# The gated layer of a four-layer transformer kernel: the logistic function in one ScalarE operation

## What is computed

```python
x1 = x + attn_out
h2 = _rms_norm(x1, ln2_w)
mlp = jax.nn.silu(h2 @ w_gate) * (h2 @ w_up) @ w_down
processed = x1 + mlp
gate = jax.nn.sigmoid(sel_scores).reshape(S, 1)
gated = gate * processed + (1.0 - gate) * x
output = hidden_states.at[b, idx].set(gated.reshape(B, k, D))
```

## Time and profile before

| | us |
|---|---|
| median of 3 runs | 1667.61 |
| the runs | 1668.44, 1667.61, 1667.5 |
| the profiled execution, its own time | 1672.15 |
| span of the profiled execution | 1670.3 |
| stage around the change, in that span | about 791 to 822 |

### The profile page before, as it was taken

How to read it: one execution, slowest core, us unless ns; L and a number is a source line. 1 busy time by engine, 2 the same in 40 slices (tenths; PEclk the granted TensorE clock), 3 DMA queues, 4 the chain that set the end, 5 groups by cost and what they waited for, 6 DMA issues and landing times. The chain is left out here.

```text
span 1670.3 us, 26603 instructions
## 1 busy us (share of the span) xinstructions
PE 1495.2 (90%) x8478; PEld 1012.7 (61%) x8540; DVE 1264.9 (76%) x3430; ACT 1108.1 (66%) x2384; POOL 1087.1 (65%) x1281
## 2 busy tenths in 40 slices
PE   7899999999999767987748999999999999987998
PEld 4334434434434236756646888878888888776675
DVE  5688788888888239642659999999999999873433
ACT  2146666666766737122238999999999999994332
POOL 6205566566565572131448999999999999963353
PEclk9779999999999979999979999999999999999999
DMA  5301001001000033821000000000000100000000
GB/s 202 114 21 39 21 21 39 21 21 40 21 22 20 2 129 109 318 101 51 0 1 1 1 1 1 1 1 1 1 1 1 51 1 1 1 1 1 1 26 26
DMA packets 39812, 59.84 MB, mean 36 GB/s; under 512 B 9132, under 2 KB 33592, under 8 KB 38776
## 3 DMA queue, kind: packets, MB, share of 16 engines
q1 hardware_dynamic: 39528, 56.03, 10.0%
q10 hardware_dynamic: 144, 2.10, 0.3%
HBM read 40.93 MB, written 16.78 MB: 35 GB/s over the span
## 5 line engine op out<-in xcount | busy, mean ns | idle before, releaser
L610 ACT ACTIVATE a_PT<-a_sc 128x512 f32<-128x512 f32 x576 | 317.7, 600 | 187.7 <-PE a_sc L678 128.4
L515 DVE TENSOR_REDUCE a_mpart<-a_nat 128x1 f32<-128x512 f32 (+3 forms) x640 | 364.3, 628 | 78.1 <-PE a_nat L645 41.0
L2057 DVE BATCH_NORM_STATS2 c_stat<-c_R 128x6 f32<-128x512 f32 x576 | 381.3, 680 | 2.0 <-ACT c_R L1976 2.0
L2021 POOL TENSOR_SCALAR c_R<-big,c_negtau 128x256 f32<-128x256 f32 x264 | 300.7, 1164 | 32.1 <-DVE c_negtau L2090 27.1
L2021 POOL TENSOR_SCALAR c_R<-c_Z,c_negtau 128x256 f32<-128x256 f32 x255 | 290.5, 1165 | 19.7 <-DVE c_negtau L2123 18.7
L642 PE MATMUL a_nat<-mem 96*128 96x512 bf16 (+3 forms) x768 | 243.6, 345 | 21.1 <-DVE a_mpart L515 10.9
L1893 PE MATMUL c_z<-mem,c_R 128*128 128x256 f32 x1024 | 231.9, 380 | 0.0
L482 POOL TENSOR_SCALAR_AFFINE_SELECT a_PT<-a_PT 128x512 f32<-128x512 f32 x128 | 79.0, 636 | 221.6 <-ACT a_PT L610 221.6
L1976 ACT ACTIVATE c_R<-c_Z,c_negtau 128x256 f32<-128x256 f32 x513 | 215.6, 513 | 0.4 <-DVE c_negtau L2123 0.4
L1976 ACT ACTIVATE c_R<-big,c_negtau 128x256 f32<-128x256 f32 x504 | 212.5, 514 | 3.1 <-DVE c_negtau L2090 1.7
L1893 PEld LDWEIGHTS c_z<-mem,c_R 128*128 128x128 f32 x1024 | 193.4, 190 | 25.6
(11 more groups left out here) (316 smaller groups left out, 2470.5 us busy)
## 6 DMA issues: line engine op xcount, KB each, us to landing
mem<-qk_parts SPq DMA_DIRECT2D x360, 32.0 KB
qk_parts<-a_parts SPq DMA_DIRECT2D x16, 384.0 KB, 2.6
made<-f_made SPq DMA_DIRECT2D x24, 256.0 KB, 2.8
mem<-made SPq DMA_DIRECT2D x3, 2048.0 KB, 7.8
X<-in_L_attn_x_dram SPq DMA_DIRECT2D x4, 512.0 KB, 6.9
mem<-in_L_ffn_wq_dram SPq DMA_DIRECT2D x1, 2048.0 KB, 14.9
ternary<-f_W_T ACTq DMA_DIRECT2D x1, 2048.0 KB, 8.3
mem<-in_L_ffn_wo_dram SPq DMA_DIRECT2D x1, 2048.0 KB, 14.1
```

The source lines that it names most:

```text
L515: dve.tensor_reduce(mpart[:, b, j:j + cnt, i, k0 // 512], src, AX.X, ALU.max).then_inc(s_max, 1)
L610: act.activation(PT[:, n % 3, c, :], sc[:, u % 2, :], ACT.Exp, scale=SCALE0).then_inc(s_exp, 1)
L2021: pool.tensor_scalar(split(i, h) if r < NR else whole(i, h), scores_of(i)[:, h, :], threshold(i, r, h), 0.0, ALU.add, ALU.max).then_inc(s_ ...
L2057: dve.bn_stats(stat[:, r, b, :], R[:, slot(i), b, :]).then_inc(s_stat, 1)
```

## The change

Unit by unit, ScalarE copies the up half first and then computes sigmoid(gate) into e1. GpSimd's addition and VectorE's reciprocal are gone, with the semaphore `s_one`. VectorE multiplies e1 by the gate into e2, and waits for product u-2 before it writes e2 again. GpSimd only makes the product with sq. The token gate gg is one Sigmoid of the router's scores; gs and its two VectorE operations are gone. The order on TensorE is the same.

```diff
@@ gpsimd
-            def one_more(u):
-                pool.wait_ge(s_eg, u + 1)
-                pool.tensor_scalar(e2[:, u % 2, :], e1[:, u % 2, :], 1.0, None, ALU.add).then_inc(s_one, 1)
-
-            one_more(0)
-            one_more(1)
             for u in range(FF1 // P):
                 pool.wait_ge(s_gate, u + 1)
                 pool.wait_ge(s_up, u + 1)
                 pool.tensor_tensor(mT[:, u, :], e2[:, u % 2, :], sq[:, u % 2, :], ALU.mult).then_inc(s_m, 1)
-                if u + 2 < FF1 // P:
-                    pool.wait_ge(s_m, u + 1)
-                    one_more(u + 2)
@@ vector
                 gate = big[:, u % 4, 0:S]
-                dve.wait_ge(s_one, u + 1)
-                c.link(dve.reciprocal(e2[:, u % 2, :], e2[:, u % 2, :]))
-                dve.wait_ge(s_up, u + 1)
-                dve.tensor_tensor(e2[:, u % 2, :], e2[:, u % 2, :], gate, ALU.mult).then_inc(s_gate, 1)
+                dve.wait_ge(s_eg, u + 1)
+                if u >= 2:
+                    dve.wait_ge(s_m, u - 1)
+                dve.tensor_tensor(e2[:, u % 2, :], e1[:, u % 2, :], gate, ALU.mult).then_inc(s_gate, 1)
 
             dve.wait_ge(s_eg, FF1 // P + 1)
-            c.link(dve.tensor_scalar(gs1[:], gs[:], 1.0, None, ALU.add))
-            c.link(dve.reciprocal(gg[:], gs1[:]))
             c.link(dve.tensor_scalar(gs1[:], gg[:], -1.0, 1.0, ALU.mult, ALU.add))
@@ scalar
-                act.activation(e1[:, u % 2, :], big[:, u % 4, 0:S], ACT.Exp, scale=-1.0).then_inc(s_eg, 1)
                 act.activation(sq[:, u % 2, :], big[:, u % 4, S:2 * S], ACT.Copy).then_inc(s_up, 1)
+                act.activation(e1[:, u % 2, :], big[:, u % 4, 0:S], ACT.Sigmoid).then_inc(s_eg, 1)
...
-            act.activation(gs[:], XS[:, :, D], ACT.Exp, scale=-1.0).then_inc(s_eg, 1)
+            act.activation(gg[:], XS[:, :, D], ACT.Sigmoid).then_inc(s_eg, 1)
```

More of the change, by code:

```diff
@@ L1324, in routed_ffn @@
         turned = mT[:].rearrange("p (e k) s -> p e k s", e=2)
-        gs, gs1, gg = sb("b1_gs", [P, B]), sb("b1_gs1", [P, B]), sb("b1_gg", [P, B])
+        gs1, gg = sb("b1_gs1", [P, B]), sb("b1_gg", [P, B])
         go = sb("b1_go", [P, B, D])
@@ L1331, in routed_ffn @@
         (s_sq, s_rs, s_h, s_tr, s_hT, s_qk, s_t, s_rope, s_v, s_vc, s_s, s_mx, s_nb, s_ex, s_rd, s_pn, s_pt, s_ptc, s_o, s_oc,
-         s_y, s_x1, s_gu, s_eg, s_dv, s_m, s_pool, s_out, s_tab, s_rot, s_et, s_etc, s_up, s_one, s_gate) = (
-            sem("b1_" + n) for n in ("sq rs h tr hT qk t rope v vc s mx nb ex rd pn pt ptc o oc y x1 gu eg dv m pool out tab rot et etc up one gate").split())
+         s_y, s_x1, s_gu, s_eg, s_dv, s_m, s_pool, s_out, s_tab, s_rot, s_et, s_etc, s_up, s_gate) = (
+            sem("b1_" + n) for n in ("sq rs h tr hT qk t rope v vc s mx nb ex rd pn pt ptc o oc y x1 gu eg dv m pool out tab rot et etc up gate").split())
         block = ctx.enter_context(nc.Block())
```

## The result

| | kernel before | changed kernel |
|---|---|---|
| median, lowest to highest (22 runs each) | 1669.44 us, 1667.40 to 1673.64 | 1666.43 us, 1665.31 to 1669.30 |
| span of the profiled execution | 1670.3 us | 1664.0 us |

The ratio of changed to before is 0.9982, 95% interval 0.9976 to 0.9988: 3.0 us less, 2.0 to 4.0. It is faster beyond the interval, but less than the 0.2% that the prediction took as its bound, so by that bound it is "same". The time of 1666.43 us lies 0.13 us above the range. Note the first column: the three runs shown ahead of the prediction had a median of 1667.61 us, the 22 runs have 1669.44.

A forecast was written before the change was run, and what follows sets the result against it. TensorE stalls behind the slower elementwise chain bounded the gated part; 1.37 + 0.14 + 0.12 + 1.95 = 3.58 us would go, leaving TensorE the bound. Off the 1667.61 us median this gave 1664.0 us, range 1662.0 to 1666.3.

The forecast's parts named there:

- the 0.2% that the prediction took as its bound: Whole kernel: a measurement can tell about 0.2%, 3.3 us, from no change; the forecast gain lay only just beyond it.
- The sum in the stage: Gated part and down product: TensorE stalls of 1.37, 0.14, 0.12 and 1.95 us all go, 3.58 us together.
- one load of 1.28 us between Copy and Sigmoid: ScalarE, first unit of the gated loop: a second function table is loaded, bounds 0 and 1.28 us, 1.28 taken.
- hidden up to 2.9 us: Before unit 4 on TensorE: a table load of up to 2.9 us is covered by TensorE's own work.
- the forecast 815.80: After the down product: VectorE's tail starts at 815.80 us instead of 819.38, earlier by 3.58.
- the same 3.58 us off the median gives 1664.0 us: Whole kernel: the stall sum of 3.58 us taken from the median of 1667.61 us gives the forecast time.
- The low stretches move with the work: TensorE's clock, as at the scatter product: assumed that low-clock stretches shift along with the work.
- a round of 4.1 us over two buffers: Gated loop: exponential, addition, reciprocal and two products form a round over two buffers, about 2.25 us a unit.
- a load back: Rival, after the gated part: the old table is reloaded on the path, at most 1.28 us, 1665.3 us; chance 0.08.
- tables to and fro: Rival, ScalarE in the gated loop: two loads in every unit, 2.57 us, giving 1674.6 us; chance 0.04.
- an elementwise chain that is hidden anyway: Rival, gated part: the change does nothing because that chain is already covered, 1667.6 us; chance 0.01.
- The clock rival: Rival, scatter product or similar pauses: clock gives or takes 1.7 us, 1662.3 or 1665.7 us; chance 0.10 for both ends.

The follow-up runs named there:

- e4: Changed kernel with the logistic function made by Tanh of half the gate, 1 added in VectorE's multiply; median 1667.40 us, ratio 0.9974 to the kernel before.
- e6: Changed kernel with a two-column Sigmoid and Exp before the first Sigmoid, so three table loads there; ratio 0.9974 to the kernel before.
- e2: Changed kernel with VectorE's reciprocal kept and only GpSimd's addition gone; ratio 0.9994 to the kernel before, stretch 22.74 us.
- e10: Kernel before (Exp, addition and reciprocal) with four buffers for e1, e2 and sq; ratio 0.9998 to the kernel before, stretch 23.69 us.
- e3: Changed kernel with an addition (of zero) kept on GpSimd and only the reciprocal gone; ratio 0.9998 to the kernel before, stretch 22.21 us.
- e9: Changed kernel with GpSimd's addition kept and four buffers for e1, e2 and sq; ratio 0.9974 to the kernel before, stretch 19.29 us.
- e5: Changed kernel with a two-column Exp after each unit's Sigmoid, 16 table loads in the gated part; ratio 1.0049 to the kernel before, stretch 31.86 us.
- e1: The changed kernel itself, run again unaltered; median 1667.09 us, ratio 0.9978 to the kernel before.
- e8: Changed kernel with ET's 16 transposes and four copies moved into TensorE's pause ahead of the gated loop; median 1662.00 us, ratio 0.9952 to the kernel before.
- e11: As the kernel with ET's transposes moved ahead, plus 16 unread transposes in each of TensorE's two pauses; median 1662.80 us, ratio 0.9959 to the kernel before.

## Why the prediction was right and wrong

**The sum in the stage was right.** It forecast that 3.58 us of stalls go and nothing takes their place; the stretch became 3.70 us shorter. Right too: one load of 1.28 us between Copy and Sigmoid, hidden up to 2.9 us (e4, e6), Sigmoid at 0.38 us, no gap in the down product, no load to bring the old table back, and the removed gs operations and the new wait at no cost. VectorE's tail came at 817.92 and not at the forecast 815.80, because in this trace unit 0 starts 0.79 us later and units 0 and 1 take 1.45 us longer; the stretch behind them is as forecast.

**The time was wrong by its base.** The step that failed is "the same 3.58 us off the median gives 1664.0 us": the mis-sized term is the base of 1667.61 us. The median of 22 runs of the same kernel is 1669.44, 1.8 us above it. This was the luck of the draw: only four of the 22 are at or below 1667.61. From 1669.44 the same sum gives 1665.86, and the measured 1666.43 is 0.57 above it. The measured gain, 3.0 us (2.0 to 4.0), holds both 3.58 and 3.70. The range had room for mechanisms, none for the base. That the base was uncertain could be read from the numbers at hand: the profiled execution took 1672.15 us, 4.5 above the median of the three runs, more than the whole forecast gain.

**"The low stretches move with the work" was wrong.** Between traces of the same code unit 0 to 2 took 4.97 to 6.62 us and the scatter 2.0 to 3.69 (table above). I had this as a rival with a chance of 0.10, as if it were one event. The traces show it as a spread of 1.7 us in each of these two places, and more behind them, so single runs differ by more than the gain, and on which side of a bound of 0.2% a gain of 3.6 us would fall was close to a coin toss.

**The reason for the stall was half right.** The prediction said that a round of 4.1 us over two buffers makes 2.25 us a unit. The pace was right, the ground was not. Two limits lay nearly side by side: VectorE with 2.12 us a unit (e2, e10), and the ring of GpSimd's queue and ScalarE, 2.46 us with the Copy in it (e3). In the kernel before, with Exp ahead of the Copy, the ring is 0.28 us shorter: the products of GpSimd ahead of and behind that of 803.09 in the earlier trace rows are 2.36 and 2.18 us from it:

```profile
800.73 0.72 POOL L1397 TENSOR_TENSOR b_mT<-b_e,b_sq 128x256 f32<-128x256 f32 x1
...
805.27 0.73 POOL L1397 TENSOR_TENSOR b_mT<-b_e,b_sq 128x256 f32<-128x256 f32 x1
```

Taking one away leaves the other: e2 gains 0.25 us in the stretch and e3 0.78, together they gain 3.70. The change works because it takes both. With the ring cut by buffers (e9), the addition costs nothing.

**The rivals.** Nothing came of a load back (two loads in all), of tables to and fro (e5 shows about its price: a stretch 8.9 us longer than before, where I had 7.0; the additional Exp of 0.2 us in each of eight units makes 1.6 of the difference), or of an elementwise chain that is hidden anyway. The clock rival, with 1.7 us either way, was real, but as a spread between traces; no run shows it as an effect of the change.

## What to carry to other kernels

Before pricing a removed operation, write down each engine's work a unit, and each ring of waits with the queue order in it; a queue that puts the work of unit u+2 ahead of that of unit u+1 turns two buffers into one. If two limits stand within 0.3 us of each other, an edit that removes one gains little, so try them together and each alone. When the effect is 0.2% of a kernel, judge it by the stretch between two fixed instructions, which repeats to 0.01 us here while the clock stays up in it, and take the base from many runs.

## What the runs showed of the hardware

- A change of ScalarE's table cost its 1283 ns with 0.01 to 0.02 us on either side, in the 16 loads of e5's units, and 1.42 us from start to start, since without a load the two operations overlap (0.28 us apart, at 0.38 us each). The Trainium skill, page "ScalarE: Activation LUTs", section "What ACT_TABLE_LOAD costs", has about 1380 ns of drain on top; between these operations, with ScalarE at work on both sides, no such time shows. The same page's section "Table sets: the hidden batching unit" is borne out: Sigmoid brought a load where Exp was active (2 loads in the changed kernel), Tanh did not (1 in e4), and Copy, Identity and Relu brought none. Square, which that section does not name, brought none either.
- TensorE's clock was at the level of 1.2 GHz behind some pauses and not behind others. Behind the pause of 2.62 us that follows the down product it was low in four traces (before, e1, e2, e9; scatter 2.46 to 3.69 us) and not in the other eight without filler (2.00 or 2.01). Ahead of unit 0, where TensorE pauses for 3.64 us in the kernel before and 1.89 in e8, it was low in all twelve traces without filler, and units 0 and 1 took 4.97 to 6.62 us. With the pause filled (e11, one trace) it stayed up, and they took 3.56. In e10 such a stretch came behind a pause of 1.4 us.
